# Where two moving operands of TensorE start in SBUF, in an attention kernel in split float32

## The reference, cut to what matters

```python
q, k, v = n @ Wq + bq, n @ Wk + bk, n @ Wv + bv      # n: x after group norm, 1024 x 256
attn = softmax((q @ k.T) * 256 ** -0.5)
out = x + (attn @ v) @ Wo + bo
```

## Time and profile before

| what | value |
|---|---|
| median of three executions | 1810.69 us |
| the profiled execution, its own time | 1810.44 us |
| its span, first to last instruction | 1808.7 us |
| PE busy | 1800.0 us, 11589 matmuls |
| PEld busy | 1643.6 us |
| DVE busy | 1662.2 us |
| ACT busy | 985.4 us |
| POOL busy | 91.2 us |

### The profile page before, as it was taken

One profiled execution on the slowest core, in us unless ns is written; L12 is line 12 of the kernel. 1 busy time (PEld: TensorE's weight loads), 2 busy tenths in 40 slices (PEclk: granted clock), 3 DMA queues, 4 the chain that ended last, 5 costly groups with the idle time before them and its releaser, 6 DMA issues.

```text
span 1808.7 us, 32719 instructions
## 1 busy us (share of the span) xinstructions
PE 1800.0 (100%) x11589; PEld 1643.6 (91%) x11589; DVE 1662.2 (92%) x2924; ACT 985.4 (54%) x1352; POOL 91.2 (5%) x106
## 2 busy tenths in 40 slices
PE   9999999999999999999999999999999999999999
PEld 8989999899998998999999989999899898999989
DVE  7999999999999999999999999999999999999997
ACT  4564554655645546556465564554654645646553
POOL 0000000000000000000000000000000000000000
PEclk9999999999999999999999999999999999999999
DMA  3221122221223202223122221122220222212201
GB/s 117 59 70 43 39 70 58 70 62 20 70 58 70 69 13 69 61 66 70 36 46 70 58 70 51 30 70 58 70 67 14 70 58 70 70 22 59 67 14 36
DMA packets 28808, 101.92 MB, mean 56 GB/s; under 512 B 3189, under 2 KB 3962, under 8 KB 28794
## 3 DMA queue, kind: packets, MB, share of 16 engines
q0 software_dynamic: 9072, 33.03, 11.7%
q1 hardware_dynamic: 19722, 68.69, 11.6%
HBM read 68.16 MB, written 66.58 MB: 74 GB/s over the span
## 4 chain that ended last, share of the span: by engine, by line
PE 96%; DVE 2%; issue 1%; ACT 1%; DMA 0%; POOL 0%; SPq 0%; DVEq 0%; POOLq 0%
PE ps_s L832 47%; PE ps_o L920 13%; PE ps_o L922 13%; PE ps_o L921 13%; PE ps_o L832 10%; DVE top L577 0%; DMA s_buf<-in_L_conv_Wk_dram 0%; DVE s_buf L607 0%; ACT s_buf L349 0%; ACT p_hi L343 0%; DVE o_buf L627 0%; DVE bn_parts L482 0%; DVE h_lo L550 0%; POOL group_stats L292 0%; ACT s_buf L335 0%
## 5 line engine op out<-in xcount | busy, mean ns | idle before, releaser
L920 PE MATMUL ps_o<-v_rows,p_hi 128*128 128x258 f32 x2048 | 581.5, 284 | 0.0
L922 PE MATMUL ps_o<-v_rows,p_lo 128*128 128x258 f32 x2048 | 576.4, 281 | 0.0
L921 PE MATMUL ps_o<-v_lo,p_hi 128*128 128x256 f32 x2048 | 574.4, 280 | 0.0
L343 ACT ACTIVATE p_hi<-s_buf 128x1024 fp32r<-128x1024 f32 x256 | 272.0, 1063 | 506.4 <-DVE s_buf L607 506.4
L832 PE MATMUL ps_s<-g_hi,h_hi 128*128 128x512 f32 x1024 | 399.3, 390 | 1.5 <-DVE v_lo L563 1.4
L832 PE MATMUL ps_s<-g_hi,h_lo 128*128 128x512 f32 x1024 | 399.0, 390 | 0.0
L832 PE MATMUL ps_s<-g_lo,h_hi 128*128 128x512 f32 x1024 | 398.8, 389 | 0.0
L921 PEld LDWEIGHTS ps_o<-v_lo,p_hi 128*128 128x128 f32 x2048 | 388.9, 190 | 2.9
L920 PEld LDWEIGHTS ps_o<-v_rows,p_hi 128*128 128x128 f32 x2048 | 385.8, 188 | 2.4
L922 PEld LDWEIGHTS ps_o<-v_rows,p_lo 128*128 128x128 f32 x2048 | 387.4, 189 | 0.0
L335 ACT ACTIVATE s_buf<-ps_s 128x512 f32<-128x512 f32 x512 | 292.8, 606 | 160.3 <-PE ps_s L832 158.8
(11 more groups left out here) (95 smaller groups left out, 2197.3 us busy)
## 6 DMA issues: line engine op xcount, KB each, us to landing
x_t<-in_x_turned_dram SPq DMA_DIRECT2D x64, 512.0 KB, 3.9
out_dram<-in_x_dram SPq DMA_DIRECT2D x63, 512.0 KB, 7.6
out_dram<-o_buf POOLq DMA_DIRECT2D x63, 512.0 KB, 5.5
x_last<-in_x_dram SPq DMA_DIRECT2D x1, 512.0 KB, 8.2
out_dram<-o_buf SPq DMA_DIRECT2D x4, 128.0 KB, 2.1
s_buf<-in_L_conv_Wq_dram SPq DMA_DIRECT2D x1, 256.0 KB, 5.0
s_buf<-in_L_conv_Wk_dram SPq DMA_DIRECT2D x1, 256.0 KB, 5.3
s_buf<-in_L_conv_Wv_dram SPq DMA_DIRECT2D x1, 256.0 KB, 5.5
```

What stands on the lines that cost most here:

```text
L343: nc.scalar.activation(p_hi[c][:, rows, :], s_buf[c][:, rows, :], ACT.Exp, scale=SCALE).then_inc(p_hi_done, 1)
L920: nc.tensor.matmul(ps[:, 0:VC], p_hi[c][:, m, cols], v_hi[:, m, :], start=m == 0, stop=False)
L921: nc.tensor.matmul(ps[:, 0:C], p_hi[c][:, m, cols], v_lo[:, m, :], start=False, stop=False)
L922: last = nc.tensor.matmul(ps[:, 0:VC], p_lo[c][:, m, cols], v_hi[:, m, :], start=False, stop=m == T - 1)
```

## The change

v_lo moves from between g_lo and shift to a place behind vo, into a padded tile of its own from element 4 on; vo_hi and vo_lo become two parts of one padded tile, from element 4 on. No instruction, size, order or semaphore is touched.

```diff
@@ -94,13 +94,15 @@
         g_lo = sb("g_lo", [P, K, N], F32R)
-        v_lo = sb("v_lo", [P, T, C], F32R)

         sb("shift", [P, 8])
         p_hi = [sb(f"p_hi{c}", [P, T, Q], F32R) for c in range(CH)]
         p_lo = [sb(f"p_lo{c}", [P, T, Q], F32R) for c in range(CH)]
-        vo_hi = sb("vo_hi", [P, K, C], F32R)
-        vo_lo = sb("vo_lo", [P, K, C], F32R)
+        vo_rows = sb("vo_rows", [P, 2 * K * C + 16], F32R)
+        vo_hi = vo_rows[:, 4:4 + K * C].rearrange("p (k n) -> p k n", k=K)
+        vo_lo = vo_rows[:, 4 + K * C:4 + 2 * K * C].rearrange("p (k n) -> p k n", k=K)
+        v_lo_rows = sb("v_lo_rows", [P, T * C + 16], F32R)
+        v_lo = v_lo_rows[:, 4:4 + T * C].rearrange("p (t n) -> p t n", t=T)
         v_rows = sb("v_rows", [P, T, VROW], F32R)
         v_hi = v_rows[:, :, 4:4 + VC]
```

## The result

The changed kernel takes 1815.32 us at the median against 1810.53 for the kernel before in the same runs, a ratio of 1.0027 with a 95% interval of 1.0018 to 1.0036: slower by 4.8 us, where 8 us less were forecast. One of its eight executions took 3623.43 us, twice the time of the others; why is not known, and the ratio leaves it out. The profiled execution took 1814.97 us, its span is 1813.3 us against 1808.7.

A forecast was written before the change was run, and what follows sets the result against it. TensorE was taken as the bound nearly everywhere. AV -8, V 0, S and G 0 from the profiled 1810.44 us made 1802.4; 1802.5 us was forecast, own range 1799.5 to 1805.5, 8-in-10 range 1797 to 1821, chance 0.43.

The forecast's parts named there:

- TensorE is the bound and only the pace can change: Whole kernel: TensorE, busy 1800.0 of 1808.7 us, waits for nobody; time is matmul count times distance between starts.
- It does what it says; VectorE and ScalarE pay nothing: The tiles land at the intended offsets; writing v_lo and vo there costs 0, at most 0.5 us.
- The mixture of 48 and 0 costs, by the excess of p_hi by v_hi over p_lo by v_hi: AV: moving operands starting 48, 0, 48 bytes past multiples of 64 cost 5.1 us, which v_lo at 48 would save.
- V's 10.2 ns as the pace of a uniform start: V's like starts leave 10.2 ns beyond columns against AV's 12.0, putting the mixed starts' cost at up to 11.1 us.
- V with vo at 48: nothing: V stages: uniform before and after, so 0 expected, bounds 2.8 us either way.
- AV: -8: AV stages with v_lo at 48: 8 us less, half way between -5.1 and -11.1; bounds -11.1 to +13.7.
- The slower rival: AV: v_lo at 48 takes in 17 stretches of 64 bytes, not 16; +8 us, 1818.5 us, chance 0.33.
- The loads set the pace: AV and V: weight loads, busy throughout, fix the pace, so moving the streams changes nothing; 1810.7 us, chance 0.24.
- Places by multiples of 64 only reorder dear and cheap matmuls: AV: v_hi and v_lo shifting by whole multiples of 64 against p would only reorder matmuls; no size of its own.

The follow-up runs named there:

- vo in the good place: Changed kernel, tiles padded wider, vo at 48 but 64 bytes further on, v_lo at 0: 1831.99 us; with v_lo also 64 bytes further on, 1830.57 us.

## Why the prediction was wrong

- *TensorE is the bound and only the pace can change.* Right for this change: the three longest waits are the same to 0.1 us, and the stages add up to the difference.
- *It does what it says; VectorE and ScalarE pay nothing.* Right: VectorE's time moved by 0.2 us.
- *The mixture of 48 and 0 costs, by the excess of p_hi by v_hi over p_lo by v_hi.* This is the step that failed. The excess of 5.1 us was read as the price of the step from 48 to 0, which v_lo at 48 would save. Instead v_lo at 48 with nothing else moved lengthened AV from 11.448 to 11.498 us, 3.1 us in 62 stages. The excess had another source: with v_lo still at 0 and only the places new, 2.9 us of the 581.5 went; in pace, the 1.5 ns that this matmul lost came back in the one behind it, and the stage stayed at 11.45. (The 5.1 us are also a difference of durations, which don't tell the pace; by starts the excess was 3.4 ns, 7 us.) A single matmul's pace in a triple that repeats tells which of the three carries a delay, not what causes it.
- *V's 10.2 ns as the pace of a uniform start.* The second measure failed too: V at 48 is as uniform as at 32 and takes 5.68 us, at 32 but 64 bytes on 5.76. The 10.2 ns were a property of one place.
- *V with vo at 48: nothing.* Mis-sized: +2.3 us, within its bound of 2.8.
- *AV: -8.* Measured +3.4 us, within the bounds of -11.1 to +13.7, on the rival's side.
- *The slower rival.* Its sign was right and its mechanism, the number of 64-byte stretches, fell with v_lo at 16 and vo at 0, so its sign was luck. Its 1818.5 was 3 us too high.
- *The loads set the pace.* AV and V changed with p, h and their loads in place, so the loads don't set the pace by themselves; h's place counts beside vo's.
- *Places by multiples of 64 only reorder dear and cheap matmuls.* Right for the places of this change (AV 11.448 for 11.443, V 5.602 for 5.610), wrong beyond it: 64 bytes made V 5.76 instead of 5.60.

What stays open is the rule. The runs show that where its tiles start changes a stage by up to 0.3 us with the same instructions, that it is the same with vo 512 bytes and v_lo and v_hi 1024 bytes further on, and that neither the start within 64, the distance of the starts within 64, nor the number of 64-byte stretches orders the numbers. The moving and the stationary tile's place both count in V; whether it is their distance or each address by itself, and whether the next moving tile counts too, was not settled.

## What to carry to other kernels

Where TensorE streams back to back, as here, moving tiles in SBUF can change each matmul by a few ns, so move one tile at a time and run a control that moves the places and keeps the starts. Don't infer a tile's ideal start from one place: try multiples of 64 as well. And read, before tuning TensorE further, how near the second engine is: here V became 0.1 us shorter in each image and the kernel 20 us longer, as two instructions of other engines changed their order.

## What the runs showed that was not expected

- Starts of float32r tiles matter at the scale of 1 to 3% of a stage: V 5.49 to 5.76 us, AV 11.36 to 11.69, S 10.89 to 11.19, with the same instructions and the full clock.
- GpSimd's power of 128 x 4 elements takes 1.03 us where it starts 0.05 us ahead of VectorE's maximum and 2.09 where it starts 0.04 us behind it. With vo in the good place every power from the third image on was a long one; why the kernel stays in that course there and recovers elsewhere was not tried.
